# Square layers split in two flag-guarded stages each, in a post-layernorm block with three-part products

## What is computed

```python
x = x + ((Q @ (K^T V)) * sqrt(3/64)) @ wo^T      # x: 1 x 4096 x 256 fp32, Q, K, V 64 wide
x = layernorm(x)
h = silu(x @ w1^T * s1) * (x @ w2^T * s2)        # 256 -> 1024
h = gelu(h @ h1^T * s_h1)                        # 1024 -> 1024, exact GELU
h = gelu(h @ h2^T * s_h2)                        # 1024 -> 1024
x = layernorm(x + h @ w3^T * s3)                 # 1024 -> 256
```

## Time and profile before

| | |
|---|---|
| median of 3 runs | 658.42 us (658.38 to 658.77) |
| profiled execution | 660.88 us, span 659.0 us |
| TensorE (PE) matmul busy | 639.4 us, 97% |
| VectorE (DVE), ScalarE (ACT), GpSimd (POOL) busy | 72%, 62%, 42% |
| DMA | 103.9 MB, mean 158 GB/s |

### The profile page before, as it was taken

How to read it: one execution, slowest core, us unless ns; L and a number is a source line. 1 busy time by engine, 2 the same in 40 slices (tenths; PEclk the granted TensorE clock), 3 DMA queues, 4 the chain that set the end, 5 groups by cost and what they waited for, 6 DMA issues and landing times.

```text
span 659.0 us, 9226 instructions
## 1 busy us (share of the span) xinstructions
PE 639.4 (97%) x3187; PEld 536.0 (81%) x3187; DVE 477.1 (72%) x713; ACT 411.3 (62%) x696; POOL 279.3 (42%) x226
## 2 busy tenths in 40 slices
PE   9989888999999999999999999999999999999995
PEld 7868676887879888888889888888888888888885
DVE  4576565798755898598755899598746799488476
ACT  5479786857863557656763457655764456666654
POOL 0367799188000466069000367059000268069024
PEclk9999998999999999999999999999999999999999
DMA  8989899953330025734330015734340005534201
GB/s 318 379 337 354 308 377 355 345 193 128 128 130 1 1 70 160 258 128 176 133 132 1 1 35 170 274 128 142 132 174 1 0 8 185 191 128 146 111 1 66
DMA packets 24370, 103.89 MB, mean 158 GB/s; under 512 B 2224, under 2 KB 3312, under 8 KB 16496
## 3 DMA queue, kind: packets, MB, share of 16 engines
q1 hardware_dynamic: 24032, 102.98, 44.1%
q10 hardware_dynamic: 288, 0.26, 0.1%
HBM read 87.51 MB, written 23.07 MB: 168 GB/s over the span
## 4 chain that ended last, share of the span: by engine, by line
PE 72%; DVE 3%; POOL 1%; issue 1%; ACT 1%; POOLq 0%; DVEq 0%; ACTq 0%
PE ps L1285 48%; PE ps L1233 13%; PE ps L1331 8%; DVE R L925 1%; DVE xr L909 1%; PE ps L1165 1%; PE ps L1153 1%; PE ps L1354 0%; ACT R L663 0%; DVE U L944 0%; POOL rstd L476 0%; POOL quarter L504 0%; ACT quarter L709 0%; POOL rstd L447 0%; POOL quarter L513 0%
## 5 line engine op out<-in xcount | busy, mean ns | idle before, releaser
L1285 PE MATMUL ps<-R,ring 128*128 128x512 f32 x1792 | 411.2, 391 | 5.3 <-issue 4.2
L1285 PEld LDWEIGHTS ps<-R,ring 128*128 128x128 f32 x1792 | 336.5, 188 | 75.7 <-issue 4.6
L925 DVE TENSOR_TENSOR R<-quarter,R 128x512 fp32r<-128x512 f32 x284 | 250.4, 903 | 69.7 <-ACT R L663 69.5
L663 ACT CAST R<-quarter 128x512 fp32r<-128x512 f32 x288 | 175.3, 615 | 31.0 <-POOL quarter L504 12.0
L1233 PE MATMUL ps<-x1T,w 128*128 128x512 f32 x512 | 119.6, 392 | 1.2 <-issue 0.6
L709 ACT ACTIVATE quarter<-U,sc 128x512 f32<-128x512 f32 x96 | 69.5, 723 | 72.9 <-DVE U L944 32.1
L1233 PEld LDWEIGHTS ps<-x1T,w 128*128 128x128 f32 x512 | 95.2, 188 | 23.4 <-ACT sg L629 1.7
L494 POOL TENSOR_TENSOR quarter<-quarter,quarter 128x512 f32<-128x512 f32 x32 | 49.2, 1538 | 103.0 <-ACT quarter L709 96.4
L629 ACT ACTIVATE sg<-ps,sc 128x512 f32<-128x512 f32 x64 | 43.9, 689 | 62.8 <-PE ps L1233 62.7
L445 POOL TENSOR_TENSOR ve<-mv,eps 128x4 f32<-128x4 f32 x14 | 5.7, 405 | 181.9 <-DVE mv L902 181.9
L679 ACT COPY U<-ps 128x512 f32<-128x512 f32 x96 | 56.3, 586 | 36.8 <-PE ps L1285 35.0
(11 more groups left out here) (84 smaller groups left out, 373.1 us busy)
## 6 DMA issues: line engine op xcount, KB each, us to landing
ring<-combos SPq DMA_DIRECT2D x56, 1024.0 KB, 4.9
combos<-unit SPq DMA_DIRECT2D x8, 1024.0 KB, 9.0
unit<-in_h1T SPq DMA_DIRECT2D x4, 1024.0 KB, 14.0
xr<-in_x_rows SPq DMA_DIRECT2D x8, 512.0 KB, 5.0
unit<-in_h2T SPq DMA_DIRECT2D x4, 1024.0 KB, 8.4
xT<-in_xT SPq DMA_DIRECT2D x7, 512.0 KB, 8.0
out<-xr SPq DMA_DIRECT2D x7, 512.0 KB, 2.9
w<-w_dram SPq DMA_DIRECT2D x3, 1024.0 KB, 7.6
```

Source lines behind the costliest of these rows:

```text
L663: nc.scalar.copy(R[slot_of(p, u)][:, 0, c, :], quarter[operand_home(p, u)][:, c, :]).then_inc(hi_done, 1)
L925: nc.vector.tensor_tensor(r[:, 1, c, :], quarter[operand_home(p, u)][:, c, :], r[:, 0, c, :].bitcast(f32), ALU.subtract).then_inc(lo_done, 1)
L1285: last = nc.tensor.matmul(ps[:, bank + j, :], w, view(R[slot_of(p, u)][:, part, k, :]), start=n in (0, 1, 5) and k == 0 and part == 0, sto ...
```

## The change

Each square layer of pair 0 is two stages: `without_sums` (products 0 and 1) and `with_sums` (products 2 to 6 and what stands between them), each with a flag of its own, so 7 flags in all. Flag 2 covers the whole units 0 to 3 and flag 3 their sums; flag 4 the whole units 4 to 7 and flag 5 their sums; flag 6 w3. TensorE sums flag 3 before the last chunk of product 0 of layer 0, flag 4 where flag 3 was (last chunk of product 6), and flag 5 before the first chunk of product 1 of layer 1. In front of the last chunk of product 1 it waits until VectorE has read the flag's bank. The looks are spread otherwise over ScalarE's list: those at the whole unit 4 and at sums 2 and 3 in the second gate block, at sums 4 in two halves, at sums 7 in layer 1 behind the high parts of product 2. combine(4) goes ahead of `differences(0, 0)`. `beside[4]` and `[5]` lie in the second halves of the rows tiles of blocks 2 and 3, so the waits for them go from the query parts (ScalarE) to `load_rows(2)` and `load_rows(3)` (SyncE). `low_x(7)` goes ahead of VectorE's wait for T1.

```diff
@@ -33,7 +33,7 @@
 BIT_ORDER = [("wq", 0), ("whole", 0), *[("w12", i) for i in range(4)], ("whole", 1), ("whole", 2), ("sums", 0), ("whole", 3),
-             ("sums", 1), ("sums", 2), ("sums", 3), ("whole", 4), ("whole", 5), ("sums", 4),
+             ("sums", 1), ("whole", 4), ("sums", 2), ("sums", 3), ("whole", 5), ("sums", 4),
              ("whole", 6), ("whole", 7), ("sums", 5), ("sums", 6), ("sums", 7), ("w3", 0), ("w3", 1)]
@@ -49,7 +49,8 @@
 Q_BETWEEN = 4
-FLAGS = 5
+
+FLAGS = 7
 Q_BANK = (4, 5, 6, 7, 5, 4, 5, 3)
@@ -110,10 +111,10 @@
         R = [sb(f"R{i}", [P, 2, KH, BLK], f32r) for i in range(SLOTS)]
+        xr_at = top[0]
         xr = sb("xr", [P, 4, TPB * E])
         x1T = [sb(f"x1T{i}", [P, 2, EC, BLK], f32r) for i in range(2)]
-        qs_at = top[0]
         qs = [sb(f"qs{i}", [P, BLK], f32r) for i in range(2)]
@@ -152,7 +153,8 @@
         unit_at = (t2_at, r_at + 2 * 16384, r_at + 2 * 16384 + 8192, u_at, u_at + 8192, w3_at, x1T_at, x1T_at + 8192)
-        beside_at = (c11_at, c11_at + 2048, c11_at + 4096, c11_at + 6144, qs_at, qs_at + 2048, sg_at + 2048, sg_at)
+        rows_at = [xr_at + 4096 * b + 2048 for b in (2, 3)]
+        beside_at = (c11_at, c11_at + 2048, c11_at + 4096, c11_at + 6144, *rows_at, sg_at + 2048, sg_at)
         unit = [over(f"unit{i}", unit_at[i], [P, 4, HALF]) for i in range(NU)]
@@ -263,8 +265,8 @@
         def flag_at(s):
-            bank = (A + 3, A, B + 3, B + 3, B)[s]
-            return ps[0:1, bank, 0:(1, BITS, BITS, BITS, 4 * BITS)[s]]
+            bank = (A + 3, A, B + 3, A + 3, B + 3, A + 3, B)[s]
+            return ps[0:1, bank, 0:(1, 4, KH, 2 * KH, KH, 2 * KH, 4 * BITS)[s]]
         block = ctx.enter_context(nc.Block())
@@ -391,6 +393,9 @@
                         sp.wait_ge(qlo_done, b + 1)
+                        if p == 0:
+                            sp.wait_ge(unit_out[b + 2], UNIT_STORED)
+                            sp.wait_ge(bits_done, n_bits("sums", b + 2))
                         load_rows(b)
@@ -427,8 +432,6 @@
                 pool.wait_ge(bits_done, n_bits("whole", i))
-                if i in (4, 5):
-                    pool.wait_ge(op_ready, 1)
                 if i >= 6:
@@ -522,12 +525,11 @@
             combine(3)
+            combine(4)
             for p in range(NP):
                     inverse_deviation(1, 2 * p)
-                else:
-                    combine(KH)
                 further_differences(p, 0)
@@ -575,14 +577,14 @@
                 act.wait_ge(unit_in[i], 16)
-                bits(unit[i][:, 0:3:2, :].bitcast(u16).rearrange("p a (n two) -> p a n two", two=2)[:, :, :, 0], 1 + i // KH, 3 * (i % KH))
+                bits(unit[i][:, 0:3:2, :].bitcast(u16).rearrange("p a (n two) -> p a n two", two=2)[:, :, :, 0], 1 + i // KH, i % KH)
             def bits_of_sums(i, parts=range(2)):
                 if 0 in parts:
-                    bits(low_halves(unit[i][:, :, :].rearrange("p a n -> p (a n)")), 1 + i // KH, 3 * (i % KH) + 1)
+                    bits(low_halves(unit[i][:, :, :].rearrange("p a n -> p (a n)")), 1 + i // KH, KH + 2 * (i % KH))
                 if 1 in parts:
-                    bits(low_halves(beside[i][:, :]), 1 + i // KH, 3 * (i % KH) + 2)
+                    bits(low_halves(beside[i][:, :]), 1 + i // KH, KH + 2 * (i % KH) + 1)
             def bits_of_w3(h):
@@ -600,8 +602,6 @@
                     act.wait_ge(q_raw, b - 1)
-                    act.wait_ge(unit_out[b + 2], UNIT_STORED)
-                    act.wait_ge(bits_done, n_bits("sums", b + 2))
                 elif b >= 4:
@@ -716,22 +716,23 @@
                     bits_of_whole(5)
+                if L == 1:
+                    bits_of_sums(7)
                 for j in range(KH):
                     hi(p, u0 + 3, j)
-                if L == 0:
-                    bits_of_sums(4)
-                    bits_of_whole(6)
                 for j in range(KH):
                     hi(p, u0 + 4, j)
+                    if L == 0 and 1 <= j <= 2:
+                        bits_of_sums(4, range(j - 1, j))
                 if L == 0:
-                    bits_of_whole(7)
+                    bits_of_whole(6)
                 for j in range(KH):
                 if L == 0:
-                    bits_of_sums(5)
+                    bits_of_whole(7)
                 if more:
@@ -742,8 +743,7 @@
                 if L == 0:
-                    bits_of_sums(6)
-                    bits_of_sums(7)
+                    bits_of_sums(5)
                 if L == 1:
@@ -755,6 +755,8 @@
                         hi(p, u0 + 9, c)
+                if L == 0:
+                    bits_of_sums(6)
                 for j in range(KH):
@@ -813,11 +815,11 @@
                     hi(0, 1, j)
-                if j == 3:
+                if j == 1:
+                    bits_of_whole(4)
+                if j == 4:
                     bits_of_sums(2)
-                if j == 5:
-                    bits_of_sums(3)
-            bits_of_whole(4)
+            bits_of_sums(3)
             for p in range(NP):
@@ -952,6 +954,10 @@
                     lo(p, u0 + 2, j)
+                    if L == 0 and j == 1:
+                        flag_out(3)
+                    if L == 1 and j == KH - 1:
+                        flag_out(5)
                 for j in range(KH + 1):
@@ -988,9 +994,9 @@
                 if L == 0:
-                    flag_out(3)
+                    flag_out(4)
                 if p == 0 and l == 1:
-                    flag_out(4)
+                    flag_out(6)
                 if l == 1 and not more:
@@ -1023,8 +1029,8 @@
             nc.vector.tensor_copy(ET[:, :, :], ps[0:D, 2, 0:D].unsqueeze(1).broadcast_to([D, 2, D])).then_inc(et_out, 1)
+            low_x(NB - 1)
             dve.wait_ge(t1_ready, 1)
-            low_x(NB - 1)
             dve.wait_ge(t1_hi, 1)
@@ -1172,11 +1178,11 @@
             def flag_sum(s):
-                pe.wait_ge(bits_done, (n_bits("wq", 0), n_bits("w12", 3), n_bits("sums", KH - 1), n_bits("sums", NU - 1), n_bits("w3", 1))[s])
-                if s == 0:
-                    at = lowf[:, 0, BITS - 1:BITS]
-                elif s < FLAGS - 1:
-                    at = lowf[:, s - 1, :]
+                pe.wait_ge(bits_done, n_bits(*(("wq", 0), ("w12", 3), ("whole", KH - 1), ("sums", KH - 1), ("whole", NU - 1),
+                                               ("sums", NU - 1), ("w3", 1))[s]))
+                if s < FLAGS - 1:
+                    row, col, n = ((0, BITS - 1, 1), (0, 0, 4), (1, 0, KH), (1, KH, 2 * KH), (2, 0, KH), (2, KH, 2 * KH))[s]
+                    at = lowf[:, row, col:col + n]
                 else:
@@ -1271,9 +1277,17 @@
                 for j in range(KH):
+                    if L == 0 and n == 0 and j == KH - 1:
+                        pe.wait_ge(h_made, 2 * HC)
+                        flag_sum(3)
                     if L == 0 and n == 6 and j == KH - 1:
                         pe.wait_ge(sum_done[0], 3)
-                        flag_sum(3)
+                        flag_sum(4)
+                    if L == 1 and n == 1 and j == 0:
+                        pe.wait_ge(add_done, n_add(0, 2, KH - 1))
+                        flag_sum(5)
+                    if L < 2 and n == 1 and j == KH - 1:
+                        pe.wait_ge(fsum_done, 4 + 2 * L)
                     bank_free(p, l, n, j)
@@ -1288,11 +1302,19 @@
             def hidden(p, l, view):
+                without_sums(p, l, view)
+                with_sums(p, l, view)
+
+            def without_sums(p, l, view):
+                product(p, l, 0, view)
+                product(p, l, 1, view)
+
+            def with_sums(p, l, view):
                 L = 2 * p + l
                 a, b = 2 * p + 2, 2 * p + 3
-                for n in range(4):
-                    product(p, l, n, view)
+                product(p, l, 2, view)
+                product(p, l, 3, view)
                 if more and l == 1:
@@ -1305,7 +1327,7 @@
                     pe.wait_ge(gelu_done, n_gelu(L, 1, 0))
-                    flag_sum(4)
+                    flag_sum(6)
                 if not more and l == 1:
@@ -1426,7 +1448,8 @@
                 l1(1, A, view, flag_side)
-            stages_from(0, (front, first_l1, lambda view: hidden(0, 0, view), lambda view: hidden(0, 1, view)))
+            stages_from(0, (front, first_l1, lambda view: without_sums(0, 0, view), lambda view: with_sums(0, 0, view),
+                            lambda view: without_sums(0, 1, view), lambda view: with_sums(0, 1, view)))
             load_flag(FLAGS - 1)
```

## The result

The changed kernel takes 668.73 us in the median (668.22 to 669.07, 4 runs), the kernel before beside it 658.40 (657.34 to 658.77, 4 runs): a ratio of 1.0159, 95% interval 1.0141 to 1.0176. 667.7 us were forecast.

The account below looks back on a forecast made before the run. A preparation of some 130 us has TensorE and the DMA queue near full; only it is touched. Terms -0.35 + 9.0 - 1.67 + 2.0 + 0.3 = +9.3 on the median 658.42 give 667.7 us, range 665.0 to 671.0.

Parts of the forecast that it names:

- The stall: Product 1 of layer two: TensorE waits at flag 5 for the late look at sums 7; +9.0 us, bounds 8.4 and 9.6.
- The ring load: Product 3 of layer one: restart near 101.2 set by the DMA queue, not TensorE; earlier products only wait longer, net 0.
- The 2.11 us of flag 2: Wait before the flag sum at 72.16 goes, but is lost waiting for product 3's ring load; net 0, bounds 0 and -2.1.
- The term: Front: low_x(7) moved ahead of the T1 wait brings the queue's stores forward; -0.35 us, bounds -0.35 and 0.
- The clock: TensorE at a lower clock after idling: +2.0 us behind the stall, +0.3 behind the ring wait (bounds 0 and +1.3).
- What the stall covers: Layer two, product 3 and the transposes: waits of 1.03 and 0.64 us vanish; -1.67 us, bounds -1.67 and 0.
- Flags and branches: Two more flag sums, loads and branches at stage starts in the square layers: 0, bounds 0 and +0.6 us.
- The branch rival: Stage start in layer two pays the last stage's 0.59 us of issue: 668.3 us; chance 5%.
- The sum: All terms together, +9.3 us against the profiled execution's 660.88; put on the median 658.42 it gives 667.7 us.
- GpSimd's chain: Faster rival: layer two's differences run 9 us earlier, so the look at sums 7 costs nothing: 656.4 us; chance 3%.
- The ring load did not come with TensorE: Rival at product 3, layer one: the queue moves with TensorE, so the 2.11 us stay won: 665.6 us; chance 10%.
- The ring load held back by `load_rows(3)`: SyncE holds it to about 122; lands by 129, hidden, else about 1 us; in a 5% rival of 669.5 us.

Follow-up runs that it names:

- e1: Changed kernel with the look at sums 7 back in layer one, the look at sums 6 moved ahead: 660.15 us, ratio 1.0009 to the kernel before.
- e2: Changed kernel with flag sum 5 before the last chunk of product 1 of layer two, not its first: 665.15 us, ratio 1.0093 to the kernel before.
- e5: Kernel before with only low_x(7) moved ahead of VectorE's wait for T1: 657.76 us, one run.
- e8: Changed kernel with 34 matmuls, results overwritten, in front of flag sum 5 to fill the stall: 666.31 us, ratio 1.0108 to the kernel before.
- e3: Kernel before with the relays of layer two's weights and w3 issued behind product 3's ring load, not in front: 656.34 us, ratio 0.9961.
- e11: Changed kernel with low_x(7) put back behind VectorE's wait for T1: 669.69 us, one run.
- e10: Kernel before with both relays behind ring load 5 and nothing else: 660.25 us, ratio 1.0017.
- e4: Changed kernel with the edits of e1 and e3 together: 655.64 us, ratio 0.9950 to the kernel before.
- e6: e4 with the store of unit 4 also issued ahead of ring load 3: 658.57 us, ratio 0.9992 to the kernel before.
- e7: e6 with flag_out(5) ahead of VectorE's low parts of product 2, layer two: 657.93 us, ratio 0.9983 to the kernel before.
- e9: Changed kernel with e1, e7's flag_out(5) edit and both relays behind ring load 5: 655.13 us, ratio 0.9938 to the kernel before.

## Why the prediction was right, step by step

*The stall.* Predicted as a look that ends at 150.20 and a product 1 at 150.5; the trace has 150.01 and 150.29. The 0.1 us for a later start of the last GELUs is not there (133.44 in both kernels). The shift of product 1 against product 0's end at 141.52 is 8.8 us, 9.0 were put down. e1 shows that it carries the loss, e2 that it follows the look's date.

*The ring load.* Right in kind: product 3 restarts when the load lands (issued at 84.31 in after, landing 16.1 us later, restart 100.49; e1, e2, e5 and e8 agree in the same way to 0.1 us, though in e5 the profile names a copy of ScalarE as what ended the wait). The 2.11 us of flag 2 were not won, as forecast. The restart moved by -0.80 us instead of -0.35. The term took the wait of 0.35 us for T1 as what the queue would gain. Up to the store of unit 1 that is so: it is issued at 45.04 in before and at 44.71 in e5. The next ring loads are 1.4 us apart (63.90 and 62.51), and they wait for the relay of the first layer's weights, which landed after 11.9 us in before and 10.8 in e5 (10.5 to 11.0 in all other profiles). So a part of the 0.8 us may be that one execution of before. The wait for T1 is itself spread, 0.18 us in e3, 1.0 in e11 and 1.2 in e10. How the move becomes the full 1 us at ring load 2 is not shown.

*The clock.* 96 matmuls take 22.07 us at full speed (e8). Behind the ring load they take 24.42 in after against 23.61 before, +0.8 where +0.3 was taken (bounds 0 and 1.3); behind the stall 23.55, +1.5 where 2.0 was taken. The two errors cancel to 0, which is luck: e11 has them the other way round, 23.61 and 24.65.

*What the stall covers.* The 1.03 and 0.64 us are gone, as forecast. What the working missed is the wait for `fsum` before the last chunk of product 1: 1.2 us as soon as the stall doesn't hide it (e1, e4, e6). In after it costs nothing.

*Flags and branches.* No gap in after: 96 matmuls run across the stage start in product 1 and 2 of layer two in one piece, and behind the filled stall of e8 such a run takes 22.07 us, the time at full speed. The last stage has 0.34 us of issue, not 0.59; over all profiles that gap is absent in two (e3, e8) and 0.31 to 0.59 in the others, so the difference is spread and not a gain. The branch rival fell. The Trainium skill's rule on taken branches ("Runtime: NRT & Kernel Launch", Instruction fetch mechanics) has a stall only where a branch is taken to a target that isn't fetched; the trace agrees in that these starts, all on the exact path, show none. No run here shows which of the branches are taken.

*The sum.* +9.3 was put against the profiled execution; there the trace has +7.7, 1.6 less: -0.45 at the restart, -0.25 at the last stage, -0.2 each for the stall and for transposes that now run without a pause, and -0.25 behind 198.10 and outside the span; some 0.25 us are not assigned. That the median moved by 10.3 and so met the forecast is helped by the 2.5 us by which the profile of before lay over its median. What made that execution longer is not shown, since the timed runs have no timeline. That the number was hit to 1.0 us is therefore in part luck; against the profiles the sum was 1.6 us too high.

*The rivals.* GpSimd's chain began at 134.31 in both kernels, so it did not come early. The ring load did not come with TensorE. The ring load held back by `load_rows(3)` was issued at 122.06, as forecast, and nothing waits for it. No wait of TensorE in after leads to the other rows and looks that were moved; e10 shows that the moved tile even takes away a wait that before would meet.

## What to carry to other kernels

A flag or a sum that a queue must evaluate in order costs the date of its last input less the date of its place; when a look is moved to make room, follow it down its new queue to what stands in front of it there, on other engines too. A gain ahead of a transfer that lands late by its queue's order is not a gain until that order is changed, and moving the backlog one step only hands the wait to the next load or store. Where waits are hidden by a larger one, list them: they come back when it is removed.

## What the runs showed of the hardware

- An idle time of 2.1 us at the flag sum near 70 left TensorE at 1.2 GHz behind it in e5 and e10 (12 matmuls in 4.41 and 4.45 us) and not in before and e3 (3.01 and 3.02 us), with the same wait. The same holds a little higher: behind 2.90 us idle e4 ran 64 matmuls in 14.76 us, behind 2.76 us e6 took 16.38. A short wait may cost 1.4 to 1.6 us more or nothing.
- Behind idle times of 3.5 to 8.5 us the slow stretch cost 1.5 to 2.9 us per stall (64 matmuls in 17.64 us in e7 against 14.76; 96 in 23.55 to 24.65 us against 22.07), and the longer idle time did not cost more: in after 8.45 us of it cost 1.5 and 5.64 us cost 2.4, and in e7 3.52 us cost 2.9.
- A 1 MB load behind two unit loads and 3 MB of relays in its queue landed after 15.9 to 16.3 us (before, after, e1, e2, e5, e8, e11). Behind the unit loads alone it took 7.8 to 10.2 (e3, e4, e9, e10), with the store of unit 4 between them 13.1 and 13.4 (e6, e7), and over all ring loads 4.9 in the median.
